# The last 64 gate columns and the last 64 up columns as one tile: eleven gate and up units a batch in place of twelve

## The reference, cut to what matters

```python
xn = _layernorm(x)
s = _L0_attn_ref(xn, Wq, Wk, Wv, Wo)          # softmax attention, then @ Wo.T
gate = silu(_qlinear(xn, wq_gate, s_gate))    # 256 -> 704
up = _qlinear(xn, wq_up, s_up)                # 256 -> 704
g = silu(_qlinear(gate * up, wq_down, s_down))  # 704 -> 256
x = x + s * g
```

## Time and profile before

| | us |
|---|---|
| median of 3 runs | 377.93 |
| the three runs | 376.08, 377.93, 378.49 |
| profiled execution | 376.7 |
| its span | 374.9 |

### The profile page before, as it was taken

One profiled execution on the slowest core, in us unless ns is written; L12 is line 12 of the kernel. 1 busy time (PEld: TensorE's weight loads), 2 busy tenths in 40 slices (PEclk: granted clock), 3 DMA queues, 4 the chain that ended last, 5 costly groups with the idle time before them and its releaser, 6 DMA issues.

```text
span 374.9 us, 5717 instructions
## 1 busy us (share of the span) xinstructions
PE 310.1 (83%) x2192; PEld 199.3 (53%) x2192; DVE 218.4 (58%) x362; ACT 168.6 (45%) x238; POOL 121.4 (32%) x183
## 2 busy tenths in 40 slices
PE   0184096779987999899999998999999999998755
PEld 0162073466654655476665554666666667564323
DVE  4762078654545599755646898637456555557212
ACT  2311163234433556445426566534346665435730
POOL 4600065321113354521014646301126564112310
PEclk9999679869998999999999999999999999999996
DMA  7628790010397500120879101005793010001101
GB/s 280 160 72 186 182 166 2 3 56 3 106 170 203 88 1 3 25 92 14 203 189 197 23 0 58 2 4 155 172 231 64 0 60 3 1 3 56 59 0 56
DMA packets 21038, 31.40 MB, mean 84 GB/s; under 512 B 2308, under 2 KB 9988, under 8 KB 21012
## 3 DMA queue, kind: packets, MB, share of 16 engines
q1 hardware_dynamic: 20740, 30.26, 33.7%
q10 hardware_dynamic: 272, 0.79, 0.6%
HBM read 20.19 MB, written 10.49 MB: 82 GB/s over the span
## 4 chain that ended last, share of the span: by engine, by line
PE 51%; DVE 23%; DMA 13%; ACT 5%; issue 3%; SPq 3%; POOL 0%; POOLq 0%; DVEq 0%; ACTq 0%
PE ps L307 11%; DMA qk_scratch<-hid 10%; PE ps L309 9%; PE ps L308 8%; PE ps L462 7%; PE ps L408 5%; PE ps L443 5%; DVE mx L851 4%; DVE mx L853 3%; PE ps L420 3%; DMA qp<-ctr 2%; DVE nw L816 2%; DVE xn L823 2%; DVE hid L839 2%; ACT hid L586 2%
## 5 line engine op out<-in xcount | busy, mean ns | idle before, releaser
L762 POOL TENSOR_SCALAR_AFFINE_SELECT pt<-pt 128x256 f32<-128x256 f32 (+1 forms) x112 | 48.5, 447 | 145.1 <-ACT pt L640 145.1
L640 ACT ACTIVATE pt<-ps 128x1024 f32<-128x1024 f32 x80 | 81.9, 1024 | 27.5 <-PE ps L443 27.4
L307 PE MATMUL ps<-xh,guh 128*128 128x512 f32 x96 | 43.6, 454 | 14.3 <-DVE hid L839 10.0
L408 PE MATMUL ps<-kp,qp 48*128 48x512 f32 (+3 forms) x256 | 37.4, 350 | 14.4 <-DVE mx L851 8.2
L851 DVE TENSOR_REDUCE mx<-ps 128x2 f32<-128x1024 f32 x32 | 39.1, 1222 | 13.0 <-PE ps L420 12.5
L748 POOL TENSOR_TENSOR hl<-hid,hh 128x512 fp32r<-128x512 f32 x24 | 32.0, 1332 | 42.2 <-ACT hh L600 41.8
L462 PE MATMUL ps<-pt,vt 128*17 128x256 f32 (+3 forms) x512 | 44.6, 444 | 0.8 <-POOL pt L762 0.8
L443 PE MATMUL ps<-qp,kp 50*128 50x512 f32 (+3 forms) x256 | 40.7, 375 | 4.9 <-ACT pt L640 2.4
L744 POOL TENSOR_TENSOR hid<-hid 128x512 f32<-128x512 f32 x24 | 30.7, 1278 | 43.2 <-DVE hid L839 27.2
L586 ACT ACTIVATE hid<-ps,hsg 128x512 f32<-128x512 f32 x24 | 16.5, 689 | 52.2 <-PE ps L309 33.0
L308 PE MATMUL ps<-xl,guh 128*128 128x512 f32 x96 | 38.6, 402 | 0.0
(11 more groups left out here) (96 smaller groups left out, 525.8 us busy)
## 6 DMA issues: line engine op xcount, KB each, us to landing
qk_scratch<-hid SPq DMA_DIRECT2D x32, 256.0 KB
qp<-qk_scratch SPq DMA_DIRECT2D x16, 256.0 KB, 5.0
kp<-qk_scratch SPq DMA_DIRECT2D x16, 256.0 KB, 6.3
qp<-qk_scratch SPq DMA_DIRECT2D x16, 128.0 KB, 5.8
kp<-qk_scratch SPq DMA_DIRECT2D x16, 128.0 KB, 7.1
xr<-in_x SPq DMA_DIRECT2D x4, 512.0 KB, 3.6
out<-xr SPq DMA_DIRECT2D x8, 256.0 KB, 2.6
xin<-in_x SPq DMA_DIRECT2D x3, 512.0 KB, 3.5
```

Of the source, the lines that this page charges most:

```text
L307: nc.tensor.matmul(dst, lh, rh, start=start, stop=False)
L408: nc.tensor.matmul(ps[:, MX + e, c:c + w], qp[part, place(b, half), col, i * P:(i + 1) * P], kp[part, place(b, half), col, 0:w], start=(z ...
L640: nc.scalar.activation(pt[:, 2 * kk:2 * kk + 2, :], ps[:, ST:ST + 2, :], ACT.Exp, scale=SCALE).then_inc(exp_done, 1)
L762: mm = nc.gpsimd.affine_select(out=diag, in_=diag, compare_op=ALU.is_ge, fill=0.0, base=0, pattern=[[0, diag.shape[1]], [1, P]], channel_m ...
```

## The change

The last 64 gate columns and the last 64 up columns become one unit. The weights lie without padding: `guh` and `gul` hold the 704 gate columns, then up columns 640 to 703, then up columns 0 to 639. Unit 10 takes 128 columns from gate column 640 on, so that its bank holds the gate's last 64 in partitions 0 to 63 and the up's last 64 in partitions 64 to 127. `NGU` = 11 replaces `2 * HT`, step 19 has no unit, and whoever handled unit 11 does so at unit 10. The last tile's operations go over 64 partitions. The rest of `hh` and `hl` in that tile is cleared once. The scales of the up half are loaded a second time, at the partitions where the half now lies (`sgu`). In the head the maxima begin one unit earlier, after unit 5.

```diff
+LAST = HT - 1
+REST = HID - LAST * P
+NGU = 2 * HT - 1
...
-    19: [("gu", 1, 11)],
+    19: [],
...
+def rows(m):
+
+    return P if m < LAST else REST
...
-        guh = sb("guh", [P, 2, KD, HIDP], F32R)
-        gul = sb("gul", [P, 2, KD, HIDP], F32R)
+
+        guh = sb("guh", [P, KD, 2 * HID], F32R)
+        gul = sb("gul", [P, KD, 2 * HID], F32R)
...
+        gu_parts = ((raw_gate[:, :, 0:HID], slice(0, HID)),
+                    (raw_up[:, :, LAST * P:HID], slice(HID, HID + REST)),
+                    (raw_up[:, :, 0:LAST * P], slice(HID + REST, 2 * HID)))
...
+            sp.dma_start(sgu[REST:, 0, :], sg[0:P - REST, :]).then_inc(sc_loaded, 16)
+            sp.dma_start(sgu[REST:, 1, :], su[0:P - REST, :]).then_inc(sc_loaded, 16)
...
-                elif kind == "gu" and n % 2 == 0:
-                    pe.wait_ge(gate_done, HT * b + n // 2 + 1)
                 elif kind == "gu":
-                    pe.wait_ge(up_done, HT * b + n // 2 + 1)
+                    if n % 2 == 0:
+                        pe.wait_ge(gate_done, HT * b + n // 2 + 1)
+                    if n % 2 or n == NGU - 1:
+                        pe.wait_ge(up_done, HT * b + n // 2 + 1)
...
+                at = m * P + (HID + REST if w else 0)
+                cols = slice(at, at + P)
                 for k in range(KD):
-                    mm = split3(ps[:, bank, :], guh[:, w, k, cols], gul[:, w, k, cols],
+                    mm = split3(ps[:, bank, :], guh[:, k, cols], gul[:, k, cols],
                                 xh[:, k, :], xl[:, k, :], k == 0, k == KD - 1)
...
+                if b == 0:
+                    pe.wait_ge(rest_zero, 2)
...
-            for n in range(2 * HT):
+            for n in range(NGU):
                 gate_up(0, n)
-                if n >= 6:
-                    maxima(0, n - 6)
-                if n == 2 * HT - 1:
+                if n >= 5:
+                    maxima(0, n - 5)
+                if n == NGU - 1:
                     transpose_c(0, 0)
...
             def up_copy(b, m):
-                act_e.wait_ge(gu_ready, 2 * (HT * b + m) + 2)
+                act_e.wait_ge(gu_ready, NGU * b + min(2 * m + 2, NGU))
...
+                src = slice(0, P) if m < LAST else slice(REST, P)
+                nc.scalar.activation(hid[0:rows(m), m % 2, 1, :], ps[src, BANK["gu", b, min(2 * m + 1, NGU - 1)], :],
+                                     ACT.Copy, scale=(sgt if m < LAST else sgu)[src, 2, m:m + 1]).then_inc(up_done, 1)
...
                     if n:
                         hidden_hi(b, n // 2 - 1)
+                    if n == NGU - 1:
+                        up_copy(b, LAST)
...
+                if kind == "gu" and n == NGU - 1:
+                    hidden(b, LAST)
...
+            for part in (hh, hl):
+                nc.vector.memset(part[REST:, LAST, :].bitcast(F32), 0.0).then_inc(rest_zero, 1)
...
-                if n >= 6:
-                    maxima(0, n - 6)
+                if n >= 5:
+                    maxima(0, n - 5)
```

More of the change, by code:

```diff
@@ L59 @@
     18: [("pv", 0, 9), ("gu", 1, 10)],
[1 row of a table removed]
[1 row of a table added]
 }
 TAIL = [("pv", 0, 10), ("pv", 0, 11), ("zt", 0, 3), ("z2", 0, 1), ("o", 0, 0), ("o", 0, 1), ("y", 0, 0), ("y", 0, 1)]
[L63 removed]
+HEAD = ([("t", 0, 0), ("t", 0, 1)] + [("qk", 0, c) for c in range(4)] + [("gu", 0, n) for n in range(NGU)]
         + [("c", 0, 0)])
+def rows(m):
+    return P if m < LAST else REST
 def step_units(b, s):
@@ L585, in gate_tanh @@
                     act_e.wait_ge(sc_step, 1)
-                nc.scalar.activation(hid[:, m % 2, 0, :], ps[:, BANK["gu", b, 2 * m], :], ACT.Tanh,
-                                     scale=hsg[:, m:m + 1]).then_inc(tanh_done, 1)
+                part = slice(0, rows(m))
+                nc.scalar.activation(hid[part, m % 2, 0, :], ps[part, BANK["gu", b, 2 * m], :], ACT.Tanh,
+                                     scale=hsg[part, m:m + 1]).then_inc(tanh_done, 1)
             def up_copy(b, m):
-                act_e.wait_ge(gu_ready, 2 * (HT * b + m) + 2)
+                act_e.wait_ge(gu_ready, NGU * b + min(2 * m + 2, NGU))
                 if b == 0 and m == 0:
                     act_e.wait_ge(sc_step, 2)
-                nc.scalar.activation(hid[:, m % 2, 1, :], ps[:, BANK["gu", b, 2 * m + 1], :], ACT.Copy,
-                                     scale=sgt[:, 2, m:m + 1]).then_inc(up_done, 1)
+                if b == 0 and m == LAST:
+                    act_e.wait_ge(sc_step, 4)
+                src = slice(0, P) if m < LAST else slice(REST, P)
+                nc.scalar.activation(hid[0:rows(m), m % 2, 1, :], ps[src, BANK["gu", b, min(2 * m + 1, NGU - 1)], :],
+                                     ACT.Copy, scale=(sgt if m < LAST else sgu)[src, 2, m:m + 1]).then_inc(up_done, 1)
             def hidden_hi(b, m):
@@ L599, in hidden_hi @@
                     act_e.wait_ge(f_ready, KD * b)
-                nc.scalar.copy(hh[:, m, :], hid[:, m % 2, 0, :]).then_inc(hhi_done, 1)
+                part = slice(0, rows(m))
+                nc.scalar.copy(hh[part, m, :], hid[part, m % 2, 0, :]).then_inc(hhi_done, 1)
             def ffn_tanh(b, d):
@@ L666, in _ @@
             nc.scalar.copy(wh[:].rearrange("p k n -> p (k n)"), raw_qkv).then_inc(wh_done, 1)
-            for w in range(2):
-                act_e.wait_ge(gu_float, w + 1)
-                nc.scalar.copy(guh[:, w].rearrange("p k n -> p (k n)"),
-                               raw_gu[:, w * KD * HIDP:(w + 1) * KD * HIDP]).then_inc(guh_done, 1)
+            for n, (raw, cols) in enumerate(gu_parts):
+                act_e.wait_ge(gu_float, min(n + 1, 2))
+                nc.scalar.copy(guh[:, :, cols], raw).then_inc(guh_done, 1)
             for k in range(KD):
@@ L836, in gate @@
             def gate(b, m):
-                a = hid[:, m % 2, 0, :]
+                part = slice(0, rows(m))
+                a = hid[part, m % 2, 0, :]
                 dve.wait_ge(tanh_done, HT * b + m + 1)
-                nc.vector.scalar_tensor_tensor(a, a, 1.0, ps[:, BANK["gu", b, 2 * m], :], ALU.add, ALU.mult
+                nc.vector.scalar_tensor_tensor(a, a, 1.0, ps[part, BANK["gu", b, 2 * m], :], ALU.add, ALU.mult
                                                ).then_inc(gate_done, 1)
```

42 lines of the change are left out of this document (23 added, 19 removed).

## The result

The changed kernel takes 384.84 us (median of four runs, 382.16 to 389.41) against 377.00 for the kernel before (375.48 to 378.49): a ratio of 1.0184, interval 1.0102 to 1.0267. I had predicted 380.2, with a range from 376.4 to 382.8. A second measurement, for which I expected 382 to 386, gave 385.38 against 377.23, ratio 1.0132 (1.0046 to 1.0217). Twenty-four matmuls fewer cost 5 to 7 us by these ratios. The profiled execution is the slowest of the four, 389.41 us, 4.6 over the median, so its rows show more low clock than a middling run has.

What follows compares the result with a forecast made beforehand. TensorE, busy 83%, waits for VectorE at the first two batch changes, so dropped matmuls gain nothing there. Terms sum to +0.24 us without a clock fall, +1.57 with one, +2.90 with two, on 377.93; predicted 380.2, range 376.4 to 382.8.

Steps and rivals of the forecast that it cites:

- the term for the clock: Batch ends, step 19 to next step 0: idle TensorE may drop to half clock, 0 to 1.33 us each.
- The naive sum: Whole kernel: four dropped units of 1.58 us all lie on the path, 6.3 us less, 371.6 us.
- Seams one and two, worth 0: Step 19 to next step 0, first two times: TensorE waits for VectorE anyway, so dropping the twelfth unit gains 0.
- Seam three, +0.38: Last batch change: scores wait for ScalarE's exponential, now behind the up copy; +0.38 us, bounds -0.06 and +0.59.
- The head, 0: 46 to 76 us: earlier maxima win time that a later gate eats; 0 us, bounds -0.6 and +0.5.
- The preparation, -0.14: Preparation of weights: low part of the gate half has 1408 columns, not 1536; 0.14 us less, small additions covered.
- rival B: Batch ends: the clock does not fall, everything else as forecast; 378.2 us, chance 0.25.
- Rival C: First two batch ends: VectorE's normalisation finishes sooner, up to 1.24 us back each; 375.1 us, chance 0.10.
- rival D: First two batch ends: GpSimd's multiplication makes VectorE's normalisation wait 1.28 us more, plus three clock falls; 384.9 us, chance 0.12.
- The sentence of the Trainium skill: First two batch ends: short idle times between matmul groups make the clock swing; falls certain at both, sum +2.90 us.

Runs made afterwards that it cites:

- old-head: The changed kernel with the head's maxima beginning after unit 6 again, as in the kernel before; 384.75 us, ratio 1.0185 to the kernel before.
- exponential-first: The changed kernel with the last tile's up copy back behind step 19's exponential and its product behind the mask; 384.11 us, ratio 1.0123 to the kernel before.
- thin unit's kernel: The kernel before with unit 11 of batches 1 to 3 as one matmul in place of six, other engines' order unchanged; 380.33 us, ratio 1.0068.

## Why the prediction was wrong

The step that failed is the term for the clock: how long a fall lasts, and so what it costs. The forecast had 1.33 us for a fall; the falls of the changed kernel's first profile cost 2.7, 3.9 and 4.0 us. Beside it, the third seam's chance of a fall was put too low, and its path by 0.33 us too short.

**The naive sum** is refuted as the forecast had it: six matmuls more at each seam made the changed kernel faster.

**Seams one and two, worth 0** without a fall: right. It is 3.93 us from tanh to maxima against 3.98, and the first seam of the second profile, which kept its clock, lost nothing.

**Seam three, +0.38:** the mechanism was right, and the rows show ScalarE's exponential as what releases the scores (2.21 us of wait). The size was not. From the tanh to scores(0) it is now 3.09 us (313.77 to 316.86), before 2.38 (305.78 to 308.16): +0.71, over my upper bound of 0.59. I took the row spacing of an ordinary activation, which overlaps its neighbour; this one does not overlap.

**The head, 0:** open, and probably too low. The walk through it was right at its start: the hole grew to 3.62 us, forecast 3.7. What was given only as a bound then happened, the clock fell behind it:

```profile
58.61 0.79 PE L431 MATMUL ps<-kp,qp 48*128 48x512 f32 x2 [3.62 <-DVE mx L888]
...
57.00:63.80 6.80, 5.19 (x21) 3.14 (x22) 3.78 (x8) 0.69 (x1) 1.97 (x2) 0.50 0.01 2
```

The first exponential was 1.4 us late in that execution and 4.7 in the second, over the bound of +0.5. But the first low stretches lie elsewhere and have other lengths in each execution, of the kernel before's head too, and taking the change in the head back moved the median by only 0.6 us (385.38 to 384.75).

**The preparation, -0.14,** is too small to be seen beside the head.

**The clock** is the term that failed, in two of its sentences. "I hold a fall at each of these seams for likely, 65%, and at the third for 30%": in the first profile all three fell, in the second two of three, the third seam among them. It fell in the old-head and the exponential-first kernels as well, so in four profiled executions of four. Its hole is 2.21 us and has 1.03 us of exponential to wait for; it is no shorter than those of the first two ahead of the scores. "A fall costs 1.33 us ... so 0 to 1.33 at each seam": this took the spell of 3.4 us at 119.7 for the only length there is. Such spells do cost that here (1.2 to 1.3 us at each seam of the thin unit's kernel), but in the changed kernel's two profiles one of five lasted 3.4 us, two 6.8 and two 10.2, and those of the first profile cost 2.7, 3.9 and 4.0. The row that said so stood outside the ones I had chosen: the kernel before has spells of 10.2 us in its head (41.2 to 51.4 and 71.9 to 82.1), and I had shown only the first third of the second. With the lengths of the profiled execution the sum is 0.24 + 0.33 (what was missing at seam three) + 2.7 + 3.9 + 4.0 = +11.2 of the 12.7 measured there; most of the other 1.5 is the head, which is 1.4 us late in that execution. For the median it is 0.57 + 7.1 by the low time of all runs at 0.39, 7.7 against 8.1, and 0.57 + 4.7, so 5.3, at 0.26. Between 0.4 and 2.8 us of the median's loss stay unexplained, and how much of the low time is the head's and how much the seams' is known only for the two profiled executions. The chances did not fit each other either: with 65, 65 and 30% for the three seams, no fall at all has a chance of 0.09 if they are independent, and rival B was given 0.25.

**Rival C** is refuted by 3.93 us, **rival D** by the rows of VectorE and GpSimd: the normalisation took 1.36 us and no second wait followed. Its 384.9 is near the measured time by accident; its mechanism did not occur. **Rival B** asked for no fall.

The sentence of the Trainium skill that I set against the change ("TensorE: Matmul & The Clock Gate", section "A second HAM failure mode: psum-queue depth-cycling") was the better forecast: short idle times between groups of matmuls did make the clock swing at these seams. I gave it a price of +2.90, since I priced it with the short spell.

What is not settled: why one spell lasts 3.4 us and another 10.2. Those of 10.2 us began at or ahead of the scores of step 0 (237.9, 316.4, and 235.1 in the old-head kernel), most of 3.4 us in the `pv` matmuls behind them (156.0, 234.5, 239.5, 314.6, 318.9). But one that began ahead of the scores (240.4 in the second profile) lasted 6.8, and so did one that began in the `pv` matmuls (159.4) and one between scores and maxima (157.6). Full-width matmuls had been running for 3.8 us before the spell of 237.9 ended. No experiment here varied this alone.

## What to carry to other kernels

A matmul that fills a wait is not free to take out: if TensorE waits for another engine there already, the time stays the same and the clock may fall behind the hole. Here that cost 0.39 us for each us at the low level where TensorE was busy throughout, and 0.26 on average over the runs. Price such a fall by the longest spell in the trace, not by the handiest. And when a unit is dropped, put the hole where TensorE and not its suppliers is late, and move everything that the last unit sets off on ScalarE, VectorE and GpSimd behind what the next step's scores and maxima need; that turned +1.8% into -1.1% with as many matmuls.

## What the hardware showed that I had not expected

The same seam of the same kernel kept its clock in one execution (131.2 to 240.4 at 1.00 in the second profile of the changed kernel) and lost it for 6.8 us in another; the second seam lost it for 10.2 and for 6.8 us. An activation that moves its data down by 64 partitions starts no sooner than its neighbour has ended (0.63 and 0.71 us between starts at durations of 0.60 and 0.68), where the copy of 128 partitions starts 0.09 us before the tanh ends (154.70 against 154.79). Whether the move does this, or reading from partition 64 on, no run tells apart. And one execution of one kernel had a granted clock of 0.65 from 100 to 395 us, neither of the two levels of the others, with TensorE busy nearly all the time; it took 443.48 us, while its nine others took 378.47 to 384.10.
